# A residual network on one core: 64 moving columns instead of 128, a scan ahead of a scale, and constants made inside the step

## The chip, the core and the metric

The kernel runs on one core of a Trainium2 chip. Time is the device time of one execution, in microseconds (us). TensorE has a clock that the chip grants at one of two levels, 2.4 or 1.2 GHz; the profile shows it as PEclk, 1.00 or 0.50 (a value between is a stretch with both).

## What is computed

The input is 8 sequences of 256 tokens with 512 features. A small network runs on each token (64 channels, 4 layers), its output is normalised and added to the input, and a second part (a router over 128 slots with the 8 best, a gate) is added after it. The change lies in the layers:

```python
h = einsum('blv,dv->bld', x, Win) + bin
def body(h, p):
    y = silu(layernorm(h, l1w, l1b))
    y = sconv(y, pr + 1j * pi, lr + 1j * li)   # a decaying complex scan along the sequence
    h = h + y * scl
    y = layernorm(h, l2w, l2b)
    y = silu(einsum('bld,fd->blf', y, w1) + b1_)
    y = einsum('blf,df->bld', y, w2) + b2_
    return (h + y, None)
```

All matmuls named below are float32, except the one that adds `b2`.

## The kernel before, in words

The 2048 tokens are 4 groups of 512 (`GROUPS`), a group is 4 tiles of 128 tokens. A **unit** `u` is one layer of one group; there are 16 (`UNITS`), and unit `u` depends on unit `u - 4`. The residual `h` of a group lives in one PSUM bank (`HK[g]`, banks 2 to 5): tile `j` has 128 columns there, of which the first 64 are `h` (`H[g]`), and the last 64 are written by the matmuls and read by nobody. The right sides of those matmuls (`wcc`, the columns from `MX0` of `cvst`, `ffst`) are 128 wide with 64 columns of zeros.

The engines run as a hand-written pipeline of **steps** `s` = 0 to 19, two of them merged into the loop that follows. In step `s` unit `s` goes through the first normalisation, unit `s - 1` through the scan and back into `h`, and unit `s - 2` through the feed-forward part. Each engine has its own list of work in each step, in program order, and waits on semaphores:

- **TensorE** (`step`, from L1111): `turn2(s-2)` transposes the normalised `h` (L1080) into bank 1 (`T2B`); `hidden(s-2)` is the first feed-forward product (L1092); `mix_in(s-1)` adds the scan's result to `h` (L1062); `turn1(s)` transposes for the first branch (L1049); `first_h(s+2)` makes `h` at the start (L1037); `project(s-2)` adds `b2` (L1100) and the second feed-forward product (L1106).
- **ScalarE** (`step`, from L463): `z_out(s-2)` copies the transposed block (L454), a square for the next step's first norm (L440), two `silu2` of `hidden` (L461), the square for the second norm of unit `s-1` (L440), then `silu1(s)` (L445).
- **VectorE** (`step`, from L772): the second `scale(s-2)` (L743), `scan(s-1)` (L762), `demodulate(s-1)` (L768), a sum of squares (L729), `scale_twice(s)` (L735), the sum of squares for the second norm of unit `s-1` (L729), `modulate(s)` (L753).
- **GpSimd** raises the sums of squares to the power -1/2 (L320), from which the scales get `RS`.

Weights of the last part are made on the way, one piece after each of the steps 4 to 10 (`LATE0` = 4, `LATES` = 7, `setup_late(0)` to `(6)`): TensorE multiplies into bank 1, the same bank that `turn2` writes (`LB` is `T2B`), and ScalarE copies it out. So `turn2` waits for that copy (`late_read`). Piece 0 feeds `wo_bias` of VectorE in step 4 (L692, L695); in step 6 VectorE also runs `score_rows` (L700 to L705).

From step 17 on come the output projection (L1133) and the second part of the network (L1144, L1157, L1202).

Of the kernel before, what the change touches and what calls it, by code (L numbers as in the profile page):

```python
# [31 lines left out]
P = 128  # L32
DEPTH, DIM, DFF, VOCAB = 4, 64, 256, 512
# [11 lines left out]
VC = VOCAB // P  # L45
# [27 lines left out]
MX0 = T20 + LEN // 2  # L73
# [8 lines left out]
def build(nc, x, xT, win, binb, ch, c64, w1d, w2t, b1, b2b, late, wu1, wr, wvu, boutr, srow, out):  # L82


    with ExitStack() as ctx:
# [8 lines left out]
        XT = sb("XT", [P, GROUPS, VC, GW])  # L94
# [20 lines left out]
        wcc = sb("wcc", [P, VC, P])  # L115
        binc = sb("binc", [P, DIM])
        cvst = sb("cvst", [P, DEPTH, NCV])
        ffst = sb("ffst", [P, DEPTH, NFF])
# [28 lines left out]
        U = sb("U", [P, GROUPS, UC])  # L147
# [3 lines left out]
        HD = sb("HD", [P, 2, 2, GW])  # L151
# [24 lines left out]
        HK = bank[2:6]  # L176
# [75 lines left out]
        LATE0, LATES = 4, 7  # L252
# [124 lines left out]
        def _(act):  # L377
# [30 lines left out]
            def setup_late(i):  # L408

                if i == 0:  # L410
                    act.activation(WOR[0:DIM, :], c6c("wout"), ACT.Copy, scale=c6c("lw"),
                                   accum_out=sm[0:DIM, 0:1]).then_inc(sums_ready, 1)
                    return
                act.wait_ge(late_mm, i + 1)
                if i == 1:
                    act.activation(rkT[:, :], LB[0:RDIM, 0:NSLOT], ACT.Copy).then_inc(late_read, 1)
                if i == 2:
                    act.activation(vpT[:, :], LB[0:VB, 0:NSLOT], ACT.Copy).then_inc(late_read, 1)
                if i == 3:
                    act.activation(KB[:, NSLOT:2 * NSLOT], c6c("keys"), ACT.Copy, scale=float(BOT) ** -0.5)  # L420
                    act.activation(KB[:, 0:NSLOT], LB[0:BOT, 0:NSLOT], ACT.Copy, scale=float(RDIM) ** -0.5) \
                        .then_inc(late_read, 1)
                if i == 4:
                    act.activation(V2R[:, :], LB[:, :], ACT.Copy, accum_out=sm[:, 1:2]).then_inc(late_read, 1)
                if i >= 5:
                    c = 2 * (i - 5)
                    act.activation(SW_[:, c:c + 2, 0:2 * NSLOT], LB[:, :].rearrange("p (c n) -> p c n", c=2),
                                   ACT.Copy).then_inc(late_read, 1)
# [27 lines left out]
            def silu2(u, a):  # L456
                g, L = u % GROUPS, u // GROUPS
                act.wait_ge(f2, u + 1)
                if u == 0:
                    act.wait_ge(ff_done, 1)  # L460
                act.activation(HD[:, u % 2, a, :].rearrange("p (h n) -> p h n", h=2), FB[a], ACT.Silu,  # L461
                               bias=ffst[:, L, 2 * P + a:2 * P + a + 1]).then_inc(g2, 1)

            def step(s):
                if s < GROUPS:
                    square(s, (h0_done, s + 1), sq1)
                ffn = 0 <= s - 2 < UNITS
                if ffn:
                    z_out(s - 2)
                if GROUPS <= s + 1 < STEPS:  # L470
                    square(s + 1, (a2, s - GROUPS + 2), sq1)
                if ffn:
                    silu2(s - 2, 0)
                    silu2(s - 2, 1)
                if 0 <= s - 1 < UNITS:
                    square(s - 1, (a1, s), sq2)
                if s < UNITS:
                    silu1(s)
                else:
                    last_z(s)  # L480
# [19 lines left out]
            for s in range(STEPS - EARLY):  # L500
                if s == 1:
                    b1_out()
                if s == LATE0 + LATES + 2:
                    setup_last()
                step(s)
                if 0 <= s - LATE0 < LATES:
                    setup_late(s - LATE0)
            def exps(k):

                act.wait_ge(am_max, k + 1)  # L510
# [53 lines left out]
        def _(dve):  # L564
# [161 lines left out]
            def sum_squares(u, squared, done):  # L726
                g = u % GROUPS
                dve.wait_ge(squared, u + 1)
                dve.tensor_reduce(SS[:, g, :], SQ[:, g, :, :], AX.X, ALU.add).then_inc(done, 1)  # L729
# [27 lines left out]
            def scan(u):  # L757
                g, L = u % GROUPS, u // GROUPS
                dve.wait_ge(u1, u + 1)
                if u == 0:  # L760
                    dve.wait_ge(cv_store, 2)
                dve.tensor_tensor_scan(V[:, g, :], cvst[:, L, DC0:DC0 + UC], U[:, g, :], 0.0, ALU.mult,  # L762
                                       ALU.add).then_inc(v1, 1)
# [8 lines left out]
            def step(s):  # L772
                conv = 0 <= s - 1 < UNITS
                if s < GROUPS:
                    sum_squares(s, sq1, ss1)
                if 0 <= s - 2 < UNITS:
                    scale(s - 2, rs2, z2)
                if conv:
                    scan(s - 1)
                    demodulate(s - 1)  # L780
                if s + 1 < GROUPS:
                    input_stats(s + 1)
                if GROUPS <= s + 1 < STEPS:
                    sum_squares(s + 1, sq1, ss1)
                if s < UNITS:
                    scale_twice(s)
                else:
                    scale(s, rs1, z1)
                if s == 1:
                    ffn_constants()  # L790
                for k in {0: (0, 1, 2, 3), 2: (4, 5), 3: (6, 7)}.get(s, ()):
                    table_level(k, 1, DEPTH)
                if conv:
                    sum_squares(s - 1, sq2, ss2)
                if s == LATE0:
                    wo_bias()
                if s == LATE0 + 2:
                    score_rows()
                if s + 1 < GROUPS:
                    first_h(s + 1)  # L800
                if s < UNITS:
                    modulate(s)
# [181 lines left out]
        def _(pe):  # L984
# [45 lines left out]
            def first_h(g):  # L1030

                pe.wait_ge(s_xt[g], 16)
                if g == 0:
                    pe.wait_ge(win_done, 1)
                for j in range(GT):
                    for c in range(VC):
                        last = pe.matmul(HK[g][:, j * P:(j + 1) * P], XT[:, g, c, j * P:(j + 1) * P],  # L1037
                                         wcc[:, c, :], start=(j == 0 and c == 0), stop=(c == VC - 1),
                                         skip_group_check=True)
                last.then_inc(h0_mm, 1)  # L1040

# [13 lines left out]
            def mix_in(u):  # L1055

                g, L = u % GROUPS, u // GROUPS
                pe.wait_ge(w1, u + 1)
                if u == 0:
                    pe.wait_ge(cv_store, 1)  # L1060
                for j in range(GT):
                    last = pe.matmul(HK[g][:, j * P:(j + 1) * P], U[:, g, j * P:(j + 1) * P],  # L1062
                                     cvst[:, L, MX0:MX0 + P], start=False, stop=True, skip_group_check=True)
                last.then_inc(a1, 1)

            def turn2(u):
# [29 lines left out]
            def project(u):  # L1096
                g, L = u % GROUPS, u // GROUPS
                if u == 0:
                    pe.wait_ge(b2_done, 1)
                pe.matmul(H[g], pick[:, :], B2W[:, L, :].unsqueeze(1).to_broadcast([ROWS, GT, DIM]), start=False,  # L1100
                          stop=True, skip_group_check=True)
                pe.wait_ge(g2, 2 * u + 2)
                for j in range(GT):
                    at = (j % 2) * HW + j // 2 * P
                    for a in range(2):
                        last = pe.matmul(HK[g][:, j * P:(j + 1) * P], HD[:, u % 2, a, at:at + P],  # L1106
                                         ffst[:, L, a * P:(a + 1) * P], start=False, stop=True,
                                         skip_group_check=True)
                last.then_inc(a2, 1)

            def step(s):  # L1111
                ffn = 0 <= s - 2 < UNITS
                if ffn:
                    turn2(s - 2)
                    hidden(s - 2)
                if 0 <= s - 1 < UNITS:
                    mix_in(s - 1)
                turn1(s)
                if s + 2 < GROUPS:
                    first_h(s + 2)  # L1120
                if ffn:
                    project(s - 2)
# [40 lines left out]
            setup_ffn()  # L1163
            for s in range(STEPS - EARLY):
                step(s)
                if 0 <= s - LATE0 < LATES:
                    setup_late(s - LATE0)
            for k in range(PAIRS + LAG):
                if k < EARLY:
                    step(STEPS - EARLY + k)  # L1170
# [87 lines left out]
```

## Time and profile before

| | |
|---|---|
| median of 3 runs | 272.15 us (272.02 to 272.39) |
| the profiled execution | 272.17 us |
| its span in the trace | 270.4 us |
| TensorE matmul busy | 206.9 us (77%) |
| TensorE weight load busy | 148.5 us (55%) |
| VectorE busy | 198.8 us (74%) |
| ScalarE busy | 116.0 us (43%) |
| GpSimd busy | 83.4 us (31%) |
| mean granted clock | 0.921 |

The span is the time from the first to the last instruction in the trace; 1.8 us of the execution lie around it. Matmuls are pipelined, so their busy time holds latency; a float32 matmul appears as two matmul instructions, each behind a weight load of its own. A clock of 0.50 stands in five stretches after the first 20 us and before the last outputs (26.0 to 32.9, 46.5 to 53.4, 63.6 to 70.4, 77.2 to 80.7 and 166.0 to 169.4).

### The profile page before, as it was taken

Reading aid. Unit: us, or ns where it says so; the run is one execution under the profiler, and the core shown is the slowest. Engines: PE = TensorE matmul, PEld = TensorE weight load, DVE = VectorE, ACT = ScalarE, POOL = GpSimd, SP = SyncE. Lnnn points to the kernel's source line nnn. Section 1 sums busy time; section 2 is a strip of 40 time slices with the busy share of each in tenths; the row PEclk is TensorE's granted clock in tenths of the full one; section 3 lists DMA queues with packets and bytes.
Section 4 is the critical chain, followed back from the end, with each engine's and each line's share of the span. In section 5 each row is a group of like instructions: output and inputs, shape, how many; then the busy total and the mean of one; then the engine's idle time right before and its main releaser. Section 6 shows DMA issues by size and latency. Waiting matters only on the chain.

```text
span 270.4 us, 3479 instructions
## 1 busy us (share of the span) xinstructions
PE 206.9 (77%) x1106; PEld 148.5 (55%) x1106; DVE 198.8 (74%) x590; ACT 116.0 (43%) x283; POOL 83.4 (31%) x119
## 2 busy tenths in 40 slices
PE   2964865875778788888888875899999999759630
PEld 2864863764567565667776751565555555323200
DVE  7897999996267866666777415677777975889994
ACT  3422111342244354445745444444324326869440
POOL 2603332324122222223332322222122120019872
PEclk9979599597779999999999997999999999999875
DMA  6999800000000000000000000000000000002436
GB/s 195 336 393 397 263 2 0 0 4 0 0 0 2 0 0 2 1 0 4 0 0 2 0 0 0 0 2 0 1 1 2 0 0 0 0 4 78 156 137 251
DMA packets 6868, 15.10 MB, mean 56 GB/s; under 512 B 897, under 2 KB 1761, under 8 KB 6338
## 3 DMA queue, kind: packets, MB, share of 16 engines
q1 hardware_dynamic: 6850, 14.88, 15.5%
q8 instruction: 9, 0.15, 0.2%
q14 instruction: 9, 0.07, 0.1%
HBM read 10.68 MB, written 4.19 MB: 55 GB/s over the span
## 4 chain that ended last, share of the span: by engine, by line
PE 43%; DVE 32%; ACT 12%; issue 6%; POOL 5%; POOLq 0%; DVEq 0%; ACTq 0%
PE bank L1157 13%; PE bank L1092 6%; PE bank L1133 6%; PE bank L1106 5%; DVE BN L710 4%; ACT HD L461 3%; POOL RS L320 3%; PE bank L1062 3%; PE bank L1080 2%; DVE SS L729 2%; ACT Z L454 2%; PE bank L1144 2%; DVE Z L743 2%; DVE XT L961 2%; DVE X L967 2%
## 5 line engine op out<-in xcount | busy, mean ns | idle before, releaser
L320 POOL TENSOR_TENSOR RS<-SS,nhalf 128x4 f32<-128x4 f32 x36 | 37.7, 1047 | 87.6 <-DVE SS L729 87.6
L1157 PE MATMUL bank<-SW_,Y 128*128 128x384 f32 x128 | 43.9, 485 | 0.0
L729 DVE TENSOR_REDUCE SS<-SQ 128x4 f32<-128x260 f32 x36 | 15.2, 421 | 26.8 <-ACT SQ L440 26.6
L1106 PE MATMUL bank<-ffst,HD 128*128 128x128 f32 x256 | 33.3, 286 | 0.7 <-ACT HD L461 0.7
L1157 PEld LDWEIGHTS bank<-SW_,Y 128*128 128x128 f32 x128 | 23.9, 190 | 17.0 <-issue 4.2
L1106 PEld LDWEIGHTS bank<-ffst,HD 128*128 128x128 f32 x256 | 32.1, 204 | 1.3 <-ACT HD L461 1.0
L461 ACT ACTIVATE HD<-bank,ffst 128x512 f32<-128x512 f32 x32 | 20.3, 684 | 16.8 <-PE bank L1092 16.8
L1092 PE MATMUL bank<-Z,w1st 64*128 64x256 f32 x128 | 19.3, 422 | 7.6 <-ACT Z L454 7.6
L440 ACT ACTIVATE SQ<-bank 128x256 f32<-128x256 f32 x36 | 13.7, 382 | 23.4 <-DVE bank L722 15.9
L1037 PE MATMUL bank<-wcc,XT 128*128 128x128 f32 x128 | 21.0, 341 | 3.3 <-DMA XT<-in_xT 2.5
L1037 PEld LDWEIGHTS bank<-wcc,XT 128*128 128x128 f32 x128 | 20.6, 256 | 3.7 <-DMA XT<-in_xT 3.7
L807 DVE SCALAR_TENSOR_TENSOR X<-bank,OR,X 128x512 f32<-128x512 f32 x16 | 11.3, 747 | 15.0 <-POOL OR L338 15.0
L1062 PE MATMUL bank<-cvst,U 128*128 128x128 f32 x128 | 21.3, 316 | 0.2 <-DVE U L768 0.2
L1062 PEld LDWEIGHTS bank<-cvst,U 128*128 128x128 f32 x128 | 17.9, 216 | 5.9 <-DVE U L768 3.6
L1133 PE MATMUL bank<-WO,ZL 128*128 128x512 f32 x32 | 17.2, 633 | 3.1 <-DVE X L807 3.1
L762 DVE TENSOR_TENSOR_SCAN V<-cvst,U 128x514 f32<-128x514 f32 x16 | 19.5, 1219 | 0.0
L1080 PE MATMUL bank<-ident,Z 128*128 128x128 f32 x32 | 6.9, 296 | 15.2 <-DVE Z L743 11.6
L1092 PEld LDWEIGHTS bank<-Z,w1st 64*128 64x128 f32 x128 | 11.5, 194 | 12.2 <-ACT Z L454 11.4
L454 ACT ACTIVATE Z<-bank 128x256 f32<-128x256 f32 x16 | 6.1, 384 | 26.7 <-PE bank L1080 26.7
L1049 PE MATMUL bank<-ident,Z 128*128 128x128 f32 x64 | 11.6, 312 | 7.5 <-DVE Z L735 7.5
L1202 PE MATMUL bank<-V,U 128*128 128x512 f32 x32 | 16.7, 655 | 0.7 <-ACT U L520 0.7
L497 ACT ACTIVATE V<-bank 128x128 f32<-128x128 f32 x16 | 4.3, 277 | 28.4 <-PE bank L1157 28.4
(222 smaller groups left out, 387.9 us busy)
## 6 DMA issues: line engine op xcount, KB each, us to landing
XT<-in_xT SPq DMA_DIRECT2D x4, 1024.0 KB, 13.7
X<-in_x SPq DMA_DIRECT2D x4, 1024.0 KB, 15.5
out<-X SPq DMA_DIRECT2D x8, 512.0 KB, 2.8
w1r<-in_w1d SPq DMA_DIRECT2D x1, 514.0 KB, 9.2
lt<-in_late SPq DMA_DIRECT2D x1, 385.5 KB, 14.8
c<-in_c SPq DMA_DIRECT2D x1, 301.5 KB, 10.1
w2r<-in_w2t SPq DMA_DIRECT2D x1, 256.0 KB, 13.7
SW_<-in_wu SPq DMA_DIRECT2D x1, 256.0 KB
```

The costliest lines, as they stand in the source:

```text
L320: pool.tensor_tensor(RS[:, g, :], SS[:, g, :], nhalf[:, :], ALU.pow).then_inc(done, 1)
L440: act.activation(SQ[:, g, :, 0:DIM], H[g], ACT.Square, scale=float(DIM) ** -0.5).then_inc(done, 1)
L461: act.activation(HD[:, u % 2, a, :].rearrange("p (h n) -> p h n", h=2), FB[a], ACT.Silu, bias=ffst[:, L, 2 * P + a:2 * P + a + 1]).then_in ...
L729: dve.tensor_reduce(SS[:, g, :], SQ[:, g, :, :], AX.X, ALU.add).then_inc(done, 1)
L762: dve.tensor_tensor_scan(V[:, g, :], cvst[:, L, DC0:DC0 + UC], U[:, g, :], 0.0, ALU.mult, ALU.add).then_inc(v1, 1)
L1037: last = pe.matmul(HK[g][:, j * P:(j + 1) * P], XT[:, g, c, j * P:(j + 1) * P], wcc[:, c, :], start=(j == 0 and c == 0), stop=(c == VC - 1 ...
L1062: last = pe.matmul(HK[g][:, j * P:(j + 1) * P], U[:, g, j * P:(j + 1) * P], cvst[:, L, MX0:MX0 + P], start=False, stop=True, skip_group_ch ...
L1092: last = pe.matmul(FB[a][:, h, :], w1st[h * DIM:(h + 1) * DIM, L, a * P:(a + 1) * P], Z2[h * DIM:(h + 1) * DIM, g, :], start=True, stop=True)
L1106: last = pe.matmul(HK[g][:, j * P:(j + 1) * P], HD[:, u % 2, a, at:at + P], ffst[:, L, a * P:(a + 1) * P], start=False, stop=True, skip_gr ...
L1133: pe.matmul(OB[t % 2][:, :], ZL[:, t // GT, (t % GT) * P:(t % GT + 1) * P], WO[:, :], start=True, stop=True).then_inc(o_mm, 1)
L1157: last = pe.matmul(SBK[t % 4][:, 0:SW], XNT[:, t % 4, c * P:(c + 1) * P], SW_[:, c, :], start=False, stop=(c == VC - 1))
L1202: pe.matmul(MB[t % 4][:, :], ET[:, t // 2 % 2, (t % 2) * P:(t % 2 + 1) * P], V2[:, :], start=True, stop=True).then_inc(aux_mm, 1)
```

## The change

Three edits. The matmuls into the residual (`first_h`, `mix_in`, `project`) read and write 64 columns instead of 128, and the weights on their stationary side stay 128 x 128. VectorE runs `scan(s-1)` before `scale(s-2)`, where it ran it behind. `setup_late` moves into the step: on TensorE between `hidden` and `mix_in`, on ScalarE between the two `silu2` and the square; before, it stood behind the whole step.

```diff
@@ ScalarE, step(s)
                 if ffn:
                     silu2(s - 2, 0)
                     silu2(s - 2, 1)
+                if 0 <= s - LATE0 < LATES:
+                    setup_late(s - LATE0)
                 if 0 <= s - 1 < UNITS:
                     square(s - 1, (a1, s), sq2)
@@ ScalarE, loop over the steps
                 step(s)
-                if 0 <= s - LATE0 < LATES:
-                    setup_late(s - LATE0)
@@ VectorE, step(s)
+                if conv:
+                    scan(s - 1)
                 if 0 <= s - 2 < UNITS:
                     scale(s - 2, rs2, z2)
                 if conv:
-                    scan(s - 1)
                     demodulate(s - 1)
@@ TensorE, first_h, mix_in, project
-                        last = pe.matmul(HK[g][:, j * P:(j + 1) * P], XT[:, g, c, j * P:(j + 1) * P],
-                                         wcc[:, c, :], start=(j == 0 and c == 0), stop=(c == VC - 1),
+                        last = pe.matmul(HK[g][:, j * P:j * P + DIM], XT[:, g, c, j * P:(j + 1) * P],
+                                         wcc[:, c, 0:DIM], start=(j == 0 and c == 0), stop=(c == VC - 1),
-                    last = pe.matmul(HK[g][:, j * P:(j + 1) * P], U[:, g, j * P:(j + 1) * P],
-                                     cvst[:, L, MX0:MX0 + P], start=False, stop=True, skip_group_check=True)
+                    last = pe.matmul(HK[g][:, j * P:j * P + DIM], U[:, g, j * P:(j + 1) * P],
+                                     cvst[:, L, MX0:MX0 + DIM], start=False, stop=True, skip_group_check=True)
-                        last = pe.matmul(HK[g][:, j * P:(j + 1) * P], HD[:, u % 2, a, at:at + P],
-                                         ffst[:, L, a * P:(a + 1) * P], start=False, stop=True,
+                        last = pe.matmul(HK[g][:, j * P:j * P + DIM], HD[:, u % 2, a, at:at + P],
+                                         ffst[:, L, a * P:a * P + DIM], start=False, stop=True,
@@ TensorE, step(s)
                 if ffn:
                     turn2(s - 2)
                     hidden(s - 2)
+                if 0 <= s - LATE0 < LATES:
+                    setup_late(s - LATE0)
                 if 0 <= s - 1 < UNITS:
                     mix_in(s - 1)
@@ TensorE, loop over the steps
                 step(s)
-                if 0 <= s - LATE0 < LATES:
-                    setup_late(s - LATE0)
```

The lines of the changed kernel are one or two higher than before (`scan` is L763, the second `scale` L744, `mix_in` L1064).

VectorE in the middle of the layers, one step from `modulate` to `modulate`, before (`Z` 128x256 is the second scale, the row with `V` is the scan, which this list calls by its instruction's form):

```order
L753 TENSOR_TENSOR U<-Y,cvst 128x514
L743 TENSOR_TENSOR Z<-bank,RS 128x256
L762 SCALAR_TENSOR_TENSOR V<-cvst,U 128x514
L768 TENSOR_TENSOR U<-V,cvst 128x512
L729 TENSOR_REDUCE SS<-SQ 128x4
L735 TENSOR_TENSOR Z<-bank,RS 128x512
L729 TENSOR_REDUCE SS<-SQ 128x4
```

and in the changed kernel:

```order
L754 TENSOR_TENSOR U<-Y,cvst 128x514
L763 SCALAR_TENSOR_TENSOR V<-cvst,U 128x514
L744 TENSOR_TENSOR Z<-bank,RS 128x256
L769 TENSOR_TENSOR U<-V,cvst 128x512
L730 TENSOR_REDUCE SS<-SQ 128x4
L736 TENSOR_TENSOR Z<-bank,RS 128x512
L730 TENSOR_REDUCE SS<-SQ 128x4
```

The scan and the second scale have changed places; nothing else moved on this engine.

TensorE around piece 4 of the late constants (`wvu_s,vpT` is that piece), before:

```order
L1080 MATMUL bank<-ident,Z 128x128 x2
L1092 MATMUL bank<-Z,w1st 128x256 x4
L1062 MATMUL bank<-cvst,U 128x128 x4
L1049 MATMUL bank<-ident,Z 128x128 x4
L1100 MATMUL bank<-B2W,pick 128x4x64
L1106 MATMUL bank<-ffst,HD 128x128 x8
L1022 MATMUL bank<-wvu_s,vpT 128x512
```

and in the changed kernel:

```order
L1082 MATMUL bank<-ident,Z 128x128 x2
L1094 MATMUL bank<-Z,w1st 128x256 x4
L1024 MATMUL bank<-wvu_s,vpT 128x512
L1064 MATMUL bank<-cvst,U 128x64 x4
L1051 MATMUL bank<-ident,Z 128x128 x4
L1102 MATMUL bank<-B2W,pick 128x4x64
L1108 MATMUL bank<-ffst,HD 128x64 x8
```

The piece now stands behind `hidden` and ahead of `mix_in`, and the two matmul groups into the residual are 64 wide.

## Rows read from the trace of the kernel before

**Rows 1.** Timeline of ScalarE and VectorE, step 14 into 15 (start, us, engine, line, operation):

```profile
139.99 0.78 ACT L445 ACTIVATE Y<-bank,cvst 128x512 f32<-128x512 f32 x1
140.80 0.70 DVE L753 TENSOR_TENSOR U<-Y,cvst 128x514 f32<-128x514 f32 x1 [0.33 <-ACT Y L445]
141.59 0.42 DVE L743 TENSOR_TENSOR Z<-bank,RS 128x256 f32<-128x256 f32 x1
141.93 1.22 DVE L762 TENSOR_TENSOR_SCAN V<-cvst,U 128x514 f32<-128x514 f32 x1
```

**Rows 2.** The chain that ended last, one round of it (start, us, what):

```profile
134.36 0.44 DVE SS L729
...
134.86 1.02 POOL RS L320
...
135.90 0.44 DVE Z L743
...
136.38 0.45 PE bank L1080 x2
...
136.86 0.39 ACT Z L454
...
137.29 1.16 PE bank L1092 x8
...
138.48 1.27 ACT HD L461 x2
```

**Rows 3.** Timeline of TensorE, `turn2` at its start in several steps:

```profile
63.19 0.44 PE L1080 MATMUL bank<-ident,Z 128*128 128x128 f32 x2 [3.06 <-DVE Z L743]
...
75.33 0.44 PE L1080 MATMUL bank<-ident,Z 128*128 128x128 f32 x2 [2.68 <-DVE Z L743]
...
90.94 0.44 PE L1080 MATMUL bank<-ident,Z 128*128 128x128 f32 x2 [1.31 <-DVE Z L743]
...
97.42 0.41 PE L1080 MATMUL bank<-ident,Z 128*128 128x128 f32 x2 [0.65 <-ACT KB L421]
...
104.78 0.41 PE L1080 MATMUL bank<-ident,Z 128*128 128x128 f32 x2 [0.87 <-ACT V2R L424]
...
119.33 0.41 PE L1080 MATMUL bank<-ident,Z 128*128 128x128 f32 x2 [0.78 <-ACT SW_ L427]
...
125.00 0.44 PE L1080 MATMUL bank<-ident,Z 128*128 128x128 f32 x2 [0.22 <-DVE Z L743]
...
147.76 0.44 PE L1080 MATMUL bank<-ident,Z 128*128 128x128 f32 x2 [0.23 <-DVE Z L743]
```

**Rows 4.** The chain again, in step 9, with a piece of the constants:

```profile
106.80 1.09 PE bank L1062 x8
107.89 0.44 PE bank L1049 x4
...
110.22 1.07 PE bank L1026 x4
111.31 0.61 ACT SW_ L427
```

**Rows 5.** Two stretches of TensorE by line, L997 and L1037 (length, matmul busy, weight load busy, clock, DMA):

```profile
21.32:23.26 1.94, 1.94 (x16) 1.86 (x16) 1.00 1.01 378
...
38.40:42.14 3.74, 3.73 (x32) 3.54 (x32) 1.00 0.00 0
```

**Rows 6.** Timeline of VectorE: `wo_bias` in step 4, and step 6 around `score_rows`:

```profile
72.69 0.69 DVE L692 TENSOR_TENSOR WOR<-bank,WOR 1x512 f32<-1x512 f32 x1 [3.63 <-PE bank L1005]
...
86.83 0.42 DVE L729 TENSOR_REDUCE SS<-SQ 128x4 f32<-128x260 f32 x1 [1.48 <-ACT SQ L440]
...
89.86 0.69 DVE L753 TENSOR_TENSOR U<-Y,cvst 128x514 f32<-128x514 f32 x1
```

**Rows 7.** From the start of `hidden` to the square, steps 4 and 14 (length, matmul busy, clock, DMA):

```profile
64.10:68.20 4.10, 4.10 (x18) 0.50 0.00 0
137.29:139.63 2.34, 2.33 (x19) 1.00 0.00 0
```

## The prediction

> **What bounds the kernel now.** The page says TensorE 77% busy and VectorE 74%, which settles nothing, so I read the chain that ended last, then the timeline of one step, then how often `turn2` starts. In the quiet middle of the layers (steps 12 to 16) one round of the chain is this [rows 2]: sum of squares 0.44 us, power on GpSimd 1.02, second scale 0.44, `turn2` 0.45, `z_out` 0.39, `hidden` 1.16, the two `silu2` 1.27, and then the square of the next unit, which stands behind them in ScalarE's list. With small gaps a round takes 5.69: `turn2` starts at 125.00 and, four rounds later, at 147.76 [rows 3]. Neither `mix_in` nor `project` is on it. VectorE and TensorE both have slack there, but the reader should see where VectorE's slack lies: the second scale starts at 141.59, right behind `modulate` (140.80 + 0.70 = 141.50), because the power has just come; the scan starts behind it, off the chain [rows 1].
>
> In steps 7 to 10 `turn2` doesn't wait for the scale but for ScalarE's copy of a piece of the constants (`ACT KB`, `V2R`, `SW_` behind the arrow, [rows 3]). There the chain runs through TensorE's whole list: `mix_in` 1.09, `turn1` 0.44, `project`, then the piece 1.07 and its copy 0.61 [rows 4], 7.28 to 7.36 a round.
>
> **Narrow matmuls: nothing.** [...] Sixteen matmuls of L997 with a single moving column take 1.94 us at full clock, less 0.25 of latency at the end and over 15 intervals: 0.113 each; thirty-two of L1037 with 128 columns take 3.74, so 0.112 each [rows 5]. From 1 to 128 columns the interval is that of the weight load; 64 lie between. Ends of the range: 0, and half an interval of 0.112 for each instruction. At the second end `mix_in` (8 instructions) is 0.45 shorter at full clock and 0.9 at half clock; that counts only where `mix_in` ends last, in steps 4 and 8 to 10: 3 x 0.45 + 0.9, about 2.2 us. `project` and `first_h` are off the chain in the changed order. I take 0, since the L997 row is the same case carried further.
>
> The Trainium skill (TensorE: Matmul & The Clock Gate, Back-to-back issue gap) gives an isolated gap that is N columns over the clock, by which halving N halves it, and says in the same place that in a stream of weight loads and matmuls both set the spacing. By the first alone the sum would be some 2.2 us lower; the L997 row goes with the second.
>
> **Scan ahead of the scale: 1.09 a round.** The scan needs `modulate`, which ends at 141.50; it would start at about 141.53. The scale then starts one scan later, 1.22 less 0.08 by which independent instructions on VectorE overlap in [rows 1] (141.93 against 141.59 + 0.42): 142.67 to 142.68, where it started at 141.59. The delay of 1.09 goes on to `turn2`, `z_out`, `hidden`, `silu2`, the square, and from there by `silu1` to the next `modulate`: nothing in the round absorbs it, since the scan itself moves with it. A round becomes 5.69 + 1.09 = 6.78. What the scan gains by coming earlier (0.4) goes to `demodulate` and `mix_in`, which had slack. Bounds for this term: 0 if the power came more than a scan later than `modulate` (it comes 0.09 later), 1.22 with no overlap.
>
> **Constants in mid-step.** Count from the start of `turn2`, 104.78 in step 9. `mix_in` follows `hidden` at 106.80, that is at 2.02 [rows 3, 4]. Before, the tail of the round was piece, copy and a 0.14 gap. Now the piece (1.07) runs behind `hidden` beside the `silu2`, and `mix_in` runs from 3.09 to 4.18. ScalarE's copy ends before that (`silu2` to 3.3, copy 0.6), so the square starts at 4.20, where a quiet round has 3.25. `turn1` ends 0.44 behind `mix_in`, at 4.62; `silu1` 0.78, `modulate` 0.70 and the gaps [rows 1] bring the scan to 6.18, the scale to 7.32 and `turn2` to 7.80. Without the scan edit it would have been 6.6, against 7.3 now: the edit by itself is worth 0.65 a round, and the scan takes it back and more. A small piece (steps 5 and 7) puts only its copy, about 0.3, ahead of the square: 6.78 + 0.33 = 7.11.
>
> Step 4: VectorE waited 3.63 us for piece 0, queued behind `project` [rows 6]. That goes. In its place the piece stands ahead of `mix_in`, stretched by the half clock there as the rest is (4.10 to 2.34 [rows 7]): about 1.9, and the scan costs 1.14: -3.63 + 1.9 + 1.14 = -0.6. Entering step 4 the scale is late by about 0.2, because `table_level` keeps VectorE busy before it. In steps 0 to 3 VectorE is nearly full and its order doesn't change its sum; I cost them at nothing, and if that is wrong it is by a few tenths. Step 6: the sum of squares comes at 4.62, `score_rows` puts `modulate` 3.03 later as now [rows 6], at 7.65 (7.70 with the gap); then 0.73, the scan 1.14, scale to `turn2` 0.47: 10.0.
>
> **The sum**, `turn2` to `turn2`, now [rows 3] and then:
> - entering step 4: +0.2
> - step 4: 12.14 to 11.55, -0.6
> - steps 5 and 6: 15.61 to 7.1 + 10.0, +1.5
> - step 7: 6.48 to 7.11, +0.6
> - step 8 (starts at 97.42): 7.36 to 7.80, +0.45
> - steps 9 and 10: 14.55 to 15.60, +1.05
> - step 11: 5.67 to 6.78, +1.1
> - steps 12 to 15: 22.76 to 27.12, +4.4
>
> Together +8.7. From step 17 on nothing is touched. 272.17 of the profiled execution, which is within 0.02 of the median, gives 280.9. Its own range is 277.5 to 284: below it the 2.2 of the matmuls and a little more, above it a half-clock stretch or two (step 5 had one in `mix_in`, worth 0.9, that I have let go, because a piece now fills the gap ahead of it).
>
> **Rival 1: the clock falls.** TensorE keeps full clock from 80.7 to 166.0, with idle gaps of 0.2 and 0.5 us in a quiet round. The changed round has 1.1 us more idle and streams half the columns in `mix_in` and `project`, 24 of its 39 instructions. The clock fell at 77.2 after a stretch in which TensorE idled 2.7 us and then only transposed and ran `hidden`. If it now falls inside the layers, the stretch from `hidden` to the square takes 4.10 instead of 2.34 [rows 7], +1.78 a round. In every second of the twelve rounds from step 5 on: +10.7, so 291.6. In each: +21.4, 302.3; more if `project` at half clock also catches up with `turn2`. For it: that idle time and the thin columns. Against it: measured in busy time the new round is still two thirds full, and waiting for weights may count as work. No row shows thin matmuls over a long stretch.
>
> The Trainium skill (same page, Part 1) says that the clock follows how busy the engine has recently been; it doesn't say whether an interval filled by the weight load counts. The trace agrees that clock falls come behind idle stretches and leaves the question open.
>
> **Rival 2: faster.** The constants give what they promise and the scan is free. In steps 7 to 10 `turn2` now waits for ScalarE, with the scaled Z ready before [rows 3]; if that stayed so, the scan could slip in at no cost. Without the scan's charge in steps 4 to 15 (12 x 1.09 = 13.1) the time is 267.8. It decides where the scan costs less than 0.4 a round. Against it: the same edit takes away the wait that would hide it, and steps 11 to 15 never had it.
>
> **Rival 3: the columns count after all**, 280.9 - 2.2 = 278.7. Against it [rows 5]. The change does otherwise what it says; the order of both engines shows it.
>
> **Numbers.** About 0.2% (0.54 us) is what a measurement can tell from no change. Forecast 280.9: 0.48. Rival 1: 0.38. Rival 2, faster: 0.08. Gains and losses that cancel: 0.03. Rival 3: 0.03, slower too. So faster 0.08, same 0.03, slower 0.89. The range is 276 to 304: it leaves out rival 2, the cancelling case, and the part of rival 1 in which the clock stays low throughout (0.08).
>
> **What would show it.** In the profile after: `turn2` every 6.8 us in steps 12 to 16, with the scan right behind `modulate` and the scale starting 1.1 later; 0.11 us per instruction of L1064 and L1108; no wait of 3.6 us in step 4; `turn2` waiting for VectorE, never for ScalarE. Wrong if the quiet round stays at 5.7, if those matmuls go at 0.06, or if PEclk shows 0.50 between 85 and 165 us.

## The result: 319 us, and the profile after

The changed kernel takes 319.25 us (318.62 to 320.4, 4 runs), the one before 272.27; the ratio is 1.172, with a 95% interval of 1.167 to 1.177. It is slower, as forecast, but by 47 us where the forecast said 9, and outside the range. The forecast is wrong.

The page of the changed kernel, busy time and the clock row in 40 slices:

```profile
PE 275.2 (87%) x1106; PEld 207.2 (65%) x1106; DVE 197.1 (62%) x590; ACT 117.4 (37%) x283; POOL 85.2 (27%) x119
...
PEclk9999999999999999999999999999999999997995
...
PE 62%; DVE 23%; ACT 7%; issue 3%; POOL 2%; POOLq 0%; DVEq 0%; ACTq 0%
```

TensorE is busy 68 us longer with the same 1106 instructions, none of which moves more columns than before. The costliest groups of instructions (busy us, mean ns of one, idle before):

```profile
L1108 PEld LDWEIGHTS bank<-ffst,HD 128*128 128x128 f32 x256 | 56.5, 333 | 1.6 <-ACT HD L461 0.6
L1108 PE MATMUL bank<-ffst,HD 128*128 128x64 f32 x256 | 56.4, 415 | 0.2 <-ACT HD L461 0.2
L1161 PE MATMUL bank<-SW_,Y 128*128 128x384 f32 x128 | 43.9, 485 | 0.0
L1094 PE MATMUL bank<-Z,w1st 64*128 64x256 f32 x128 | 33.2, 671 | 7.6 <-ACT Z L454 7.6
```

`project` (L1108) went from 33.3 to 56.4 us. But `hidden` (L1094), which the change didn't touch, went from 19.3 to 33.2 as well, and the scores (L1161), late in the program, stand at 43.9 as before. That looks like a slower clock in the layers, and the page's PEclk row denies it: 9 in the first 36 of its 40 slices. One round of the chain decides it (start, us, what), against [rows 2]:

```profile
152.57 2.08 PE bank L1094 x8
154.65 1.90 PE bank L1064 x8
156.54 0.85 PE bank L1051 x4
157.40 0.21 PE bank L1102
157.61 3.31 PE bank L1108 x16
160.92 0.44 PE bank L1082 x2
...
161.38 0.39 ACT Z L454
```

The round takes 9.25 us (from 152.57 to the next `hidden` at 161.82, 0.44 after `z_out` starts). It is TensorE's own list from end to end, but for the 0.47 in which TensorE waits for `z_out`. `hidden` takes 2.08. At 2.4 GHz it takes 1.16 [rows 2], and in step 4 of the kernel before, where the clock is recorded at 0.50, it takes the 2.08 as well:

```profile
64.10 2.08 PE L1092 MATMUL bank<-Z,w1st 64*128 64x256 f32 x8 [0.47 <-ACT Z L454]
```

The sixteen matmuls of `project` in that round (length, matmul busy, weight load busy, clock as printed):

```profile
157.40:160.92 3.52, 3.52 (x16) 3.33 (x16) 1.00 0.00 0
```

One matmul lasts 0.42 here (the 415 ns above), so the intervals are (3.52 - 0.42) / 15 = 0.21 each, nearly twice the 0.112 of [rows 5]. The trace holds no clock record before 213 us, and where none is, the page prints full clock. So the row of nines is an absence, not a measurement. All fourteen profiles of this case agree on what the absence means: the first record is always a stretch at the higher level. It begins at 10 to 14 us in the ten kernels whose `first_h` has 128 columns (at 12.4 in the kernel before), at 39 and 53 us in the two profiles with `first_h` alone thin, and at 213 and 216 us in the two with all three groups thin. What has no record is the time before the first rise. Another execution of the changed kernel, at 320.4 us, has a mean clock of 0.794 where the other three have 0.970 to 0.980: more of its low time is on record, and it takes nearly as long. **TensorE ran at 1.2 GHz from its first matmuls until 213 us, shortly before the scores.**

Where the 47.6 us of span went, by the starts of `turn2` (they were 63.19, 125.00 and 147.76 before [rows 3]):

```profile
64.95 0.64 PE L1082 MATMUL bank<-ident,Z 128*128 128x128 f32 x2
...
151.46 0.64 PE L1082 MATMUL bank<-ident,Z 128*128 128x128 f32 x2
...
188.45 0.63 PE L1082 MATMUL bank<-ident,Z 128*128 128x128 f32 x2
```

1.8 us were lost by step 4, 24.7 in steps 4 to 11, 14.2 in steps 12 to 15 (3.56 a round), and 6.9 from step 16 to the end. `turn2` waits for nothing before it in these rows: it is reached late by TensorE itself. Only in four of the sixteen units does it still wait for the second scale, 2.3 us in all.

### The profile page after: what moved, and what is told of

The parts are those of the page before. It is cut to its first block, busy times and chain, and to the rows that moved or that the text cites. A ratio compares the mean times of both kernels' runs of the same rounds, so it can differ in the third digit from the quotient of the medians.

```text
span 318.0 us, 3479 instructions
## 1 busy us (share of the span) xinstructions
PE 275.2 (87%) x1106; PEld 207.2 (65%) x1106; DVE 197.1 (62%) x590; ACT 117.4 (37%) x283; POOL 85.2 (27%) x119
## 4 chain that ended last, share of the span: by engine, by line
PE 62%; DVE 23%; ACT 7%; issue 3%; POOL 2%; POOLq 0%; DVEq 0%; ACTq 0%
PE bank L1108 14%; PE bank L1161 11%; PE bank L1094 10%; PE bank L1064 8%; PE bank L1137 4%; DVE BN L711 3%; PE bank L1051 3%; PE bank L1082 2%; PE bank L1204 2%; ACT Z L454 2%; DVE V L763 2%; PE bank L1148 2%; ACT U L516 1%; PE bank L1028 1%; DVE bank L723 1%
## 5 line engine op out<-in xcount | busy, mean ns | idle before, releaser
L1108 PEld LDWEIGHTS bank<-ffst,HD 128*128 128x128 f32 x256 | 56.5, 333 | 1.6 <-ACT HD L461 0.6
L1108 PE MATMUL bank<-ffst,HD 128*128 128x64 f32 x256 | 56.4, 415 | 0.2 <-ACT HD L461 0.2
L1161 PE MATMUL bank<-SW_,Y 128*128 128x384 f32 x128 | 43.9, 485 | 0.0
L1094 PE MATMUL bank<-Z,w1st 64*128 64x256 f32 x128 | 33.2, 671 | 7.6 <-ACT Z L454 7.6
L1064 PEld LDWEIGHTS bank<-cvst,U 128*128 128x128 f32 x128 | 28.5, 328 | 10.7 <-issue 10.7
L1161 PEld LDWEIGHTS bank<-SW_,Y 128*128 128x128 f32 x128 | 23.9, 190 | 17.0 <-issue 4.2
L1064 PE MATMUL bank<-cvst,U 128*128 128x64 f32 x128 | 31.4, 427 | 0.0
L1039 PE MATMUL bank<-wcc,XT 128*128 128x64 f32 x128 | 28.0, 420 | 3.6 <-DMA XT<-in_xT 2.8
L1039 PEld LDWEIGHTS bank<-wcc,XT 128*128 128x128 f32 x128 | 27.7, 332 | 4.0 <-DMA XT<-in_xT 4.0
L1094 PEld LDWEIGHTS bank<-Z,w1st 64*128 64x128 f32 x128 | 18.9, 320 | 16.8 <-ACT Z L454 14.0
L763 DVE TENSOR_TENSOR_SCAN V<-cvst,U 128x514 f32<-128x514 f32 x16 | 19.6, 1228 | 0.4
L445 ACT ACTIVATE Y<-bank,cvst 128x512 f32<-128x512 f32 x16 | 12.5, 779 | 11.4 <-PE bank L1051 11.4
L754 DVE TENSOR_TENSOR U<-Y,cvst 128x514 f32<-128x514 f32 x16 | 11.1, 694 | 8.9 <-ACT Y L445 8.9
```

The source lines that it names most:

```text
L1039: last = pe.matmul(HK[g][:, j * P:j * P + DIM], XT[:, g, c, j * P:(j + 1) * P], wcc[:, c, 0:DIM], start=(j == 0 and c == 0), stop=(c == VC ...
L1064: last = pe.matmul(HK[g][:, j * P:j * P + DIM], U[:, g, j * P:(j + 1) * P], cvst[:, L, MX0:MX0 + DIM], start=False, stop=True, skip_group_ ...
L1094: last = pe.matmul(FB[a][:, h, :], w1st[h * DIM:(h + 1) * DIM, L, a * P:(a + 1) * P], Z2[h * DIM:(h + 1) * DIM, g, :], start=True, stop=True)
L1108: last = pe.matmul(HK[g][:, j * P:j * P + DIM], HD[:, u % 2, a, at:at + P], ffst[:, L, a * P:a * P + DIM], start=False, stop=True, skip_gr ...
L1161: last = pe.matmul(SBK[t % 4][:, 0:SW], XNT[:, t % 4, c * P:(c + 1) * P], SW_[:, c, :], start=False, stop=(c == VC - 1))
```

## The experiments

### The three edits apart

The first four runs take the edits one by one and in one pair. The first puts the 128 columns back and leaves the other two edits in:

```diff
-    last = pe.matmul(HK[g][:, j * P:j * P + DIM], U[:, g, j * P:(j + 1) * P],
-                     cvst[:, L, MX0:MX0 + DIM], ...
+    last = pe.matmul(HK[g][:, j * P:(j + 1) * P], U[:, g, j * P:(j + 1) * P],
+                     cvst[:, L, MX0:MX0 + P], ...
```

and likewise in `first_h` and `project`.

> The changed kernel with the 64 moving columns put back to 128; the scan ahead of the scale and the constants in mid-step stay. Theory A (the thin matmuls keep TensorE's clock at 1.2 GHz, and that is what went wrong): the clock rises again, intervals of mix_in and project 0.112 us in the layers, a quiet round 6.78 us, and the time is that of my sum, 280.9 us (277 to 285). Theory B (the order of the steps starves TensorE, and the clock falls from its idle time, whatever the columns): about 319 us, quiet round 9.2 us. Theory C (a thin matmul into PSUM is slower by itself, the clock has nothing to do with it): also about 281 us here, but then turn2 and hidden, which nothing narrowed, must have been slow in the changed kernel for another reason.

Measured: 282.05 us, ratio 1.036 (1.028 to 1.045). Putting zeros back gains 37 us. VectorE in two rounds of this run (start, us):

```profile
136.47 0.70 DVE L754 TENSOR_TENSOR U<-Y,cvst 128x514 f32<-128x514 f32 x1 [0.33 <-ACT Y L445]
137.20 1.23 DVE L763 TENSOR_TENSOR_SCAN V<-cvst,U 128x514 f32<-128x514 f32 x1
138.35 0.40 DVE L744 TENSOR_TENSOR Z<-bank,RS 128x256 f32<-128x256 f32 x1
...
143.22 0.70 DVE L754 TENSOR_TENSOR U<-Y,cvst 128x514 f32<-128x514 f32 x1 [0.33 <-ACT Y L445]
143.95 1.23 DVE L763 TENSOR_TENSOR_SCAN V<-cvst,U 128x514 f32<-128x514 f32 x1
145.09 0.40 DVE L744 TENSOR_TENSOR Z<-bank,RS 128x256 f32<-128x256 f32 x1
```

`modulate`, scan, scale, each behind the other: the round is 6.75 (143.22 - 136.47), where I had 6.78. Theories B and C are out. B would leave the round at 9.2, and C has no reason for the slow `hidden` of the changed kernel.

The second has only the constants in mid-step (128 columns, scan behind the scale):

> Only the constants in mid-step; scan behind the scale and 128 columns as before. By my terms: steps 7 to 10 lose 0.65 us each, step 4 about 1.7, steps 5 and 6 a little: 267.8 us (266 to 270), quiet round 5.69, turn2 never waits for ScalarE. Rival: the piece ahead of mix_in delays the square by as much as it saves behind project: 272.2 us.

Measured: 266.39 us, ratio 0.977 (0.967 to 0.987). The chain in step 10, which has a piece as step 9 has (start, us, what), against [rows 4]:

```profile
107.00 0.46 PE bank L1081 x2
...
107.92 1.14 PE bank L1093 x8
109.05 0.86 PE bank L1027 x4
109.91 1.09 PE bank L1063 x8
111.00 0.45 PE bank L1050 x4
...
111.47 0.79 ACT Y L445
...
112.28 0.69 DVE U L754
...
112.99 0.42 DVE Z L744
```

The piece (L1027) costs 0.86 between `hidden` and `mix_in`, and the copy is off the chain. The round is 6.47 (107.00 to 113.47), where it was 7.28 and I had 6.6. It ends by way of `turn1`, `silu1` and `modulate`.

The third has only the scan ahead of the scale:

> Only the scan ahead of the scale. By my terms a quiet round takes 6.78 us instead of 5.69, five of them, and steps 4 and 6 pay 1.1 to 1.3 each; in steps 5 and 7 to 10 turn2 waits for ScalarE anyway and the scan is hidden: 272.2 + 8.2 = 280.4 us (278 to 282). Rival: the scan is charged nowhere, since VectorE has slack: 272.2.

Measured: 284.87 us (282.02 to 286.12), ratio 1.045 (1.036 to 1.054); 4 us more than expected by the median and above the range of 278 to 282; 2 more by the profiled execution of 282.02, whose mean clock is 0.921 where the other three have 0.904 to 0.910. `turn2` in its profile:

```profile
117.08 0.41 PE L1082 MATMUL bank<-ident,Z 128*128 128x128 f32 x2 [0.78 <-ACT SW_ L427]
124.36 0.41 PE L1082 MATMUL bank<-ident,Z 128*128 128x128 f32 x2 [0.78 <-ACT SW_ L427]
131.08 0.44 PE L1082 MATMUL bank<-ident,Z 128*128 128x128 f32 x2 [1.28 <-DVE Z L744]
137.83 0.44 PE L1082 MATMUL bank<-ident,Z 128*128 128x128 f32 x2 [1.28 <-DVE Z L744]
```

In steps 9 and 10 the round is 7.28, the scan hidden by the wait for ScalarE; from step 12 on it is 6.75 (131.08 to 137.83). So the scan is charged where the scale is on the chain. The expectation had the wrong steps for it: step 4 costs nothing more (12.03, where it was 12.14), and steps 5 and 7, where I had the scan hidden, take 9.27 and 8.23 instead of 7.87 and 6.48, with `turn2` behind them waiting for the scale. These two steps also have 3.0 and 3.4 us more at half clock than before, so the two causes aren't told apart there.

The fourth has only the thin matmuls:

> Only the 64 moving columns, all three groups of matmuls. Theory A: the clock stays at 1.2 GHz from the first steps to the scores, intervals 0.213 us; a quiet round 9.2 us and bound by TensorE, so that the scan's place doesn't matter; steps with a piece of the constants are longer than in the changed kernel by the copy behind project: about 324 us (317 to 330). Theory B: the order is that of before, so about 272.

Measured: 325.99 us (325.52 to 327.08), ratio 1.199 (1.191 to 1.206). One edit, which removes half the columns of 512 instructions and adds nothing, costs 54 us. Beside it, the whole change at 319 is 7 us better. I read this as the constants in mid-step still paying at low clock, and the scan costing little, because TensorE is late for twelve of the sixteen `turn2`; no run has the thin matmuls with only one of these two edits.

### Which columns

The next four thin one or two groups of matmuls each; order, scan and constants are those of the kernel before. The edit is that of the change, in `mix_in` and `project`:

> 64 columns in mix_in and project, 128 in first_h; scan and constants as before. Theory A says the clock is up while first_h runs at 128 columns (to about 42 us), falls in one of the first idle stretches of the layers and doesn't come back in them: close to the run with all three thin, 318 to 326 us. If only a thin start kept the clock low, the layers would run at 2.4 GHz with intervals of 0.112 and the time would be about 272.

Measured: 324.98 us (324.29 and 325.68). In this profile the clock records are there (first slices of the page, then 16 `project` matmuls: length, matmul busy, weight load busy, clock):

```profile
PEclk9977896555555555555555555577999999997995
```

```profile
141.61:145.12 3.51, 3.51 (x16) 3.33 (x16) 0.50 0.00 0
```

From 51 to 208 us the clock is recorded at 0.50 without a break, and the 3.51 us are the 3.52 of the changed kernel, whose record is missing. That confirms the reading above. Up to 51 us the clock went up and down in this run; then it fell in the layers and came back only behind them.

Is that idleness? Stretch 130 to 160 us of the kernel before, then of this one (length, busy us with instructions of TensorE, its weight loads, VectorE, ScalarE, GpSimd, clock):

```profile
130.00:160.00 30.00, 24.74 (x192) 20.20 (x190) 18.17 (x33) 15.02 (x31) 9.37 (x11) 1.00 0.00 1
```

```profile
130.00:160.00 30.00, 27.02 (x110) 21.52 (x109) 12.48 (x20) 8.18 (x17) 5.92 (x7) 0.50 0.00 1
```

TensorE is occupied more of the time, 27.0 us of 30 against 24.7, and has the lower clock. So the busy time in the trace doesn't tell the level. It streams fewer columns, but part of that is the slow clock's own doing (110 instructions in place of 192), so this pair doesn't show which comes first. The next run does.

`first_h` alone thin:

> 64 columns in first_h alone. Theory A: intervals of 0.213 in first_h, because a stretch filled with thin matmuls doesn't raise the clock, but VectorE and the input loads hold that stretch, and the clock rises in the layers at 128 columns: 272 to 277 us. Rival: the clock, once low at the start, stays low: over 300.

The profiled execution took 271.36 us, the other 362.61 (it comes back below). The first `first_h`, in the kernel before and then in this one:

```profile
7.40 6.19 PE L1037 MATMUL bank<-wcc,XT 128*128 128x128 f32 x32 [0.84 <-DVE wcc L612]
```

```profile
7.40 7.06 PE L1038 MATMUL bank<-wcc,XT 128*128 128x64 f32 x32 [0.84 <-DVE wcc L613]
```

Both start at the same time, behind the same work, with the same weight loads. With 128 columns the clock rises at 12.4, within the group. With 64 the group goes at (7.06 - 0.42) / 31 = 0.214 to its end, as the theory says, and the first rise comes at 53 us. It costs nothing in this execution, since other work holds that stretch: `turn2` of step 3 starts at 54.64 here and at 54.66 before. From there on the layers are as before.

`mix_in` alone thin, then `project` alone thin:

> 64 columns in mix_in alone, 8 of the 39 instructions of a round. Theory A: enough columns are left in project, so the clock holds, the intervals of mix_in are 0.112 at full clock as with 128 columns, and the time is that of before within a few us (271 to 278). If a thin matmul were faster at full clock the interval would be near 0.06.

> 64 columns in project alone, 16 of the 39 instructions of a round. Theory A: most of the loss of the thin kernel is here; the clock falls behind project and comes back late or not at all: 290 to 322 us, several low stretches in the trace. If the columns of mix_in decide as much, 275 to 285.

Measured: 272.71 us (270.61 and 274.81) and 273.22 us (270.81 and 275.63), beside 271.94 of the kernel before. Neither costs anything that two executions of each can show. I had expected `project` alone, with two thirds of the missing columns, to bring most of the loss; that was wrong. The loss isn't a share for each group: one group or the other may go thin, both may not.

These two also have thin matmuls at full clock. `project` thin in the one, `mix_in` thin in the other:

```profile
139.24:141.14 1.90, 1.90 (x16) 1.76 (x16) 1.00 0.00 0
```

```profile
135.31:136.41 1.10, 1.10 (x8) 0.96 (x8) 1.00 0.00 0
```

With 128 columns the groups take 1.95 and 1.16. Half the columns take 0.05 and 0.06 us off the whole group, at its end; the interval stays at 0.11. There is nothing to gain from them even where the clock holds.

### Columns put back as work that nobody needs

```diff
@@ project(u), between the b2 matmul and the wait for g2; mix_in and project thin
+                dead = HK[g].rearrange("p (j d) -> p j d", j=GT)[:, :, DIM:P]
+                pe.matmul(dead, ident[:, :], ones[:, 0:DIM].unsqueeze(1).to_broadcast([P, GT, DIM]),
+                          start=False, stop=True, skip_group_check=True)
```

> 64 columns in mix_in and project as in the run with both thin (325 us), and in each step one more float32 matmul of 256 columns ahead of the project matmuls, into the dead columns of h's bank: work that nobody needs, which gives back a third of the columns taken away. Theory A (columns streamed decide): what is left missing is about as much as in the run with project alone thin, which kept its clock, so this one gets it back too: 5.7 to 6.2 us a quiet round, 272 to 282 us, some 45 us faster for added work. Theory D (what decides is the thin matmuls themselves, both groups together): the clock stays at 1.2 GHz and the added matmul costs about 0.9 us a round: 335 us or more.

Measured: 288.19, 301.88, 300.59 and 305.99 us, median 301.24. Added work takes 24 us off the 325, and in the profiled execution 37; the slowest of the four is still 18 below the faster one without it. Neither theory had it right: D is out, since the time falls instead of rising by 10, but A promised 272 to 282. Three stretches of the profiled execution show why (columns as above):

```profile
60.00:100.00 40.00, 34.53 (x190) 28.22 (x190) 22.66 (x40) 14.00 (x29) 9.97 (x10) 0.72 0.00 1
100.00:130.00 30.00, 26.28 (x124) 20.67 (x124) 12.51 (x21) 10.77 (x23) 5.82 (x7) 0.66 0.00 1
130.00:174.00 44.00, 39.18 (x301) 33.19 (x299) 26.75 (x46) 22.09 (x46) 13.80 (x15) 1.00 0.00 1
```

From 130 us on, in the quiet rounds, the clock is full and the round is 5.69 again. Before that it goes up and down, and the four executions spread over 18 us.

This run also says what isn't known. Per step the two thin groups lack 24 x 64 = 1536 columns, and the added matmul, which is two instructions of 256, gives back 512. The 1024 that are left missing are exactly those of `project` alone thin, which ran in 271 to 276 us where this one takes 288 to 306. So the number of columns in a step doesn't settle the level by itself. Where in the step they lie may count, or the longer steps with a piece, in which most low stretches of the layers lie here; no run separates these.

> The kernel before with the same added matmul, to price it at full clock: 0.43 us a step on TensorE, hidden by slack in the quiet steps except for 0.1 to 0.2, on the chain in steps 7 to 10: 272 + 2 to 5 us.

Measured: 275.56 us (274.63 and 276.48), ratio 1.015. The added matmul is not good for anything by itself; it costs 3.5 us at 128 columns.

### Two repeats

> 64 columns in first_h alone, once more, because its two executions gave 271 and 363 us. If a thin start alone can leave the clock low for the whole program, some of these executions lie above 310 again; if the 363 was an accident of that chip, all lie at 270 to 276.

Measured: eleven executions from 268.41 to 274.16, median of all 270.89, and one of 306.97, the profiled one. Its clock record shows a level of 0.75 where all other profiles here have 1.00. Otherwise the kernel runs as before (ratio 0.995, 0.991 to 0.999). I take that, and the 363 of the first try, for a state of the chip and not for an effect of the thin start, but that isn't shown: both are among the fourteen executions of this one kernel, and none of the kernel before reached 276. It stays open whether a thin start makes it likelier.

> The constants in mid-step alone, once more and with more rounds, to have its gain over the kernel before beyond doubt: 266 to 268 us against 271 to 273, ratio 0.975 to 0.985.

Measured: 265.47 us (263.3 to 269.77, 6 executions), ratio 0.975 (0.968 to 0.981). The constants in mid-step alone beat both kernels: 6.6 us below the kernel before, 54 below the changed one.

## Why the prediction was wrong, step by step

- **What bounds the kernel.** Right. The round of 5.69, the wait for ScalarE in steps 7 to 10, and the slack of `mix_in` and `project` are confirmed by the runs that move one thing at a time. (The 7.28 to 7.36 a round that I gave for steps 7 to 10 hold for 8 to 10; step 7 takes 6.48, as the sum has it.)
- **Narrow matmuls: nothing.** Right as to the interval (0.11 us at 64 columns and full clock), and wrong as the price of the edit. This is the step that failed: the term costed the instructions at a given clock, took the clock for given, and so put the edit at nothing. Its price is 54 us alone and 37 us within the change (319.3 against 282.05). That it is paid through the clock is shown by `hidden`, which nobody touched (2.08 in place of 1.16), and by the record of 0.50 in the run with thin steps.
- **Scan ahead of the scale: 1.09 a round.** Right: 6.75 against the 6.78 forecast in both runs that have it at full clock. In the quiet rounds of the changed kernel itself it costs nothing, because there a round of 9.25 is bound by TensorE.
- **Constants in mid-step.** Right in kind, a little low: the round with a piece is 6.47 without the scan where I had 6.6, and the edit alone gives 266.4 and 265.5 where my terms gave 267.8. The piece costs 0.86 behind `hidden`, not 1.07: at the end of a step its own latency was on the chain, and here `mix_in` starts before that has passed.
- **The sum.** For the kernel it described, with the clock as it was, it was good: 280.9 against 282.05 with 128 columns. Part of that is luck, because errors cancel. In that run's profile step 4 took 8.8 us where I had 11.55, for lack of a low-clock stretch. Steps 5, 7 and 8, which have such stretches, took 5.5 more than I had together, and from step 16 on the run was 1.8 shorter than before, where I had no change.
- **Rival 1** was the case that came, and its price failed too. I gave it 0.38, and priced it at 291.6 to 302.3 by one stretch a round, from `hidden` to the square, at +1.78 (4.10 - 2.34 is 1.76; that slip is small). Low clock throughout was named and cut off from the range. A quiet round came to 9.25, which is 2.47 above the 6.78 of my sum. At 1.2 GHz `project` takes 3.31, and TensorE's list as a whole, not the stretch to the square, becomes the bound. [rows 7] gave the factor for the whole list; I applied it to the part that was on the chain before, and wrote "more if `project` at half clock also catches up with `turn2`" without pricing it. Against my sum the changed kernel lost 1.6 us by step 4, 30.4 in steps 4 to 15 and 6.9 behind them, which gives the 319.8 of the profiled execution. I also wrote that waiting for weights may count as work. The run with `mix_in` and `project` thin has TensorE occupied 90% of the time at the low clock.
- **Rival 2 and rival 3** are out. Rival 2 falls with the rounds of 6.75 in the first and the third run; the changed kernel has no step where the scan is free because `turn2` waits for ScalarE. Rival 3 falls with the groups that are thin at full clock, whose interval stays at 0.11.
- **What would show it.** I had named PEclk 0.50 as the sign. The page showed 1.00 and the clock was low all the same. The intervals of the matmuls, which I had named too (0.11 forecast, 0.21 measured), were the sign that held.

## What to carry to other kernels

Before you cut columns from matmuls that each have a weight load of their own, look at the interval: if one moving column costs as much as 128, the cut gains nothing, and the zeros you take away may be what keeps TensorE at full clock. Price a change of clock on the engine's whole list, because at half speed it can become the bound. And an operation that has slack must not be moved ahead of one that has none, however idle its engine looks; the place of a side job (here the constants) is beside work of the other engines, which is worth 2.5% here by itself.

## What the runs showed of the hardware that I had not expected

- How long TensorE is occupied doesn't tell which clock it has: 27.0 busy us of 30 at 0.50 with thin matmuls, 24.7 of 30 at 1.00 with wide ones. In a gapless group of 32 from 7.40 us on, the clock rose at 12.4 with 128 columns and not at all within the group with 64.
- Once down, the clock can stay down through the layers: recorded at 0.50 from 51 to 208 us without a break, with `mix_in` and `project` thin.
- The loss doesn't add up group by group. Thin `mix_in` or thin `project` leaves the time at 273 us, both together give 325, and a useless matmul of 256 columns a step brings 301.
- A profile has no clock records before the first rise, here for up to two thirds of its length, and prints full clock there. `hidden` at 2.08 us where it takes 1.16 is then the better witness. The mean clock of 0.921 of the kernel before also counts its first 12.4 us as full.
- In one profile the granted clock had a third value, 0.75 in place of 1.00, with 306.97 us for a kernel that otherwise takes 271.
